# A vision tower on one core: the first attention step of the first head group written apart from the loop, in another order

## The reference

```python
h = _L0_tok_ref(...)                       # 8 batches x 256 tokens x 512, from a state space kernel
h = h + attn(_layernorm(h))                # 16 query heads, 4 key/value heads, 128 wide, window 256
h = h + ffn(_layernorm(h))                 # selected low-rank update per token

q, k, v = hidden @ w_q, hidden @ w_k, hidden @ w_v      # per head
q = q * cos + rotate_half(q) * sin                      # k likewise
probs = softmax(q @ k.T / sqrt(128) + causal_bias)
out = (probs @ v) @ w_o
```

## Time and profile before

| | |
|---|---|
| median of 3 runs | 835.1 us (834.56 to 835.16) |
| the profiled execution, its own time | 833.84 us |
| its span, first to last instruction | 832.0 us |
| PE busy | 753.5 us, 91% |
| DVE, ACT, POOL busy | 577.2, 454.5, 444.6 us |
| granted TensorE clock, mean | 0.974 |

### The profile page before, as it was taken

One profiled execution on the slowest core, in us unless ns is written; L12 is line 12 of the kernel. 1 busy time (PEld: TensorE's weight loads), 2 busy tenths in 40 slices (PEclk: granted clock), 3 DMA queues, 4 the chain that ended last, 5 costly groups with the idle time before them and its releaser, 6 DMA issues.

```text
span 832.0 us, 19710 instructions
## 1 busy us (share of the span) xinstructions
PE 753.5 (91%) x6958; PEld 685.6 (82%) x6958; DVE 577.2 (69%) x1626; ACT 454.5 (55%) x1246; POOL 444.6 (53%) x662
## 2 busy tenths in 40 slices
PE   0277877899999999999999999999999999999985
PEld 0176667899999999999999999999999989899762
DVE  7999648677766666656565566655655687777877
ACT  6644327555555656555575665555656554564420
POOL 0497826544444747444465654444747556555522
PEclk9998989899999999999999999999999999999995
DMA  9033450100010102000001020000100000000002
GB/s 208 0 67 63 86 218 27 39 1 0 0 39 2 52 1 77 0 0 0 0 8 45 10 68 0 0 0 0 52 2 1 1 2 26 25 25 25 1 25 77
DMA packets 30504, 26.48 MB, mean 32 GB/s; under 512 B 22446, under 2 KB 22830, under 8 KB 30198
## 3 DMA queue, kind: packets, MB, share of 16 engines
q1 hardware_dynamic: 30310, 25.77, 10.9%
q10 hardware_dynamic: 144, 0.07, 0.0%
HBM read 17.44 MB, written 8.39 MB: 31 GB/s over the span
## 4 chain that ended last, share of the span: by engine, by line
PE 77%; DVE 11%; POOL 5%; issue 3%; ACT 2%; DMA 1%; DVEq 0%; SPq 0%; POOLq 0%; ACTq 0%
PE bank_quad L1218 17%; PE bank_quad L1220 17%; PE bank_quad L1219 16%; PE bank_pair L1220 4%; PE bank_pair L1218 4%; PE bank_pair L1219 4%; POOL w_lo L423 2%; PE bank_pair L1361 2%; PE bank_pair L1371 1%; PE bank L1371 1%; PE bank L1375 1%; DVE bank_pair L905 1%; PE bank_quad L1314 1%; PE bank_quad L1230 1%; POOL kq_lo L493 1%
## 5 line engine op out<-in xcount | busy, mean ns | idle before, releaser
L1218 PE MATMUL bank_quad<-xt_hi,w_hi 128*128 (+1 forms) x768 | 217.2, 283 | 0.8 <-POOL w_lo L423 0.8
L1220 PE MATMUL bank_quad<-xt_lo,w_hi 128*128 (+1 forms) x768 | 214.9, 280 | 0.0
L1219 PE MATMUL bank_quad<-xt_hi,w_lo 128*128 (+1 forms) x768 | 214.8, 280 | 0.0
L987 DVE TENSOR_TENSOR kq<-bank_quad,cst 128x512 f32<-128x512 f32 (+1 forms) x96 | 57.9, 603 | 140.8 <-ACT swap L679 106.6
L489 POOL TENSOR_TENSOR swap<-swap,cst 128x512 f32<-128x512 f32 (+1 forms) x96 | 105.8, 1104 | 82.3 <-ACT swap L679 79.5
L1218 PEld LDWEIGHTS bank_quad<-xt_hi,w_hi 128*128 128x128 f32 x768 | 144.9, 189 | 2.8 <-POOL w_lo L423 1.4
L1220 PEld LDWEIGHTS bank_quad<-xt_lo,w_hi 128*128 128x128 f32 x768 | 144.7, 188 | 0.0
L1219 PEld LDWEIGHTS bank_quad<-xt_hi,w_lo 128*128 128x128 f32 x768 | 144.6, 188 | 0.0
L351 POOL TENSOR_TENSOR spare<-cst 1x1 f32<-1x1 f32 x87 | 16.6, 191 | 223.3 <-DVE rinv L1121 141.1
L719 ACT ACTIVATE sm<-sm,mx 128x128 f32<-128x128 f32 (+1 forms) x256 | 114.2, 447 | 21.5 <-DVE mx L1111 21.5
L678 ACT ACTIVATE swap<-bank_quad 64x512 f32<-64x512 f32 (+1 forms) x96 | 50.4, 524 | 125.1 <-PE bank_quad L1220 122.6
(11 more groups left out here) (265 smaller groups left out, 1883.2 us busy)
## 6 DMA issues: line engine op xcount, KB each, us to landing
mixed<-st SPq DMA_DIRECT2D x32, 128.0 KB, 2.0
out<-x SPq DMA_DIRECT2D x16, 256.0 KB, 2.0
raw<-in_w_qkv SPq DMA_DIRECT2D x8, 384.0 KB, 3.5
raw<-in_w_o SPq DMA_DIRECT2D x10, 256.0 KB, 2.7
x<-mixed SPq DMA_DIRECT2D x2, 1280.0 KB, 11.0
norm_mem<-in_w_qkv SPq DMA_DIRECT2D x6, 384.0 KB, 3.6
x<-mixed SPq DMA_DIRECT2D x3, 512.0 KB, 4.6
norm_mem<-in_w_o SPq DMA_DIRECT2D x6, 256.0 KB, 2.7
```

Of the source, the lines that this page charges most:

```text
L987: v.tensor_tensor(view(kq), src, table(cosT), ALU.mult).then_inc(kq_cos, 1)
L1218: mmul(dst, lh, rh, start=start and k == 0, stop=False, skip_group_check=True)
L1219: mmul(dst, ll, rh, start=False, stop=False, skip_group_check=True)
L1220: last = mmul(dst, lh, rl, start=False, stop=stop and k == n - 1, skip_group_check=True)
```

## The change

It takes the first run `(0, 1)` out of `RUNS[0]`, and so step 0 of group 0 out of the loop body, and writes it out on each engine ahead of `steps`; the exceptions for it in the step's functions are gone.

- PE: V of batch 0 is transposed into bank 7, between the two query pairs of batch 0, and waits only for `vt`. Keys and values of batch 1 are projected ahead of batch 0's scores. Behind the transposes of the probabilities stands one `keep_warm` matmul in bank 3, and V of batch 1 is transposed behind `attend(0)` instead of ahead of it.
- DVE: the statistics of batch 2 move ahead of the first query pair's cosine product; the low parts of keys and queries of batch 0 stand between the rotations. In step 0 the first reciprocals and V's low part come ahead of `norm_apply` for batch 2, and the statistics of batch 3 and the low parts of the probabilities come ahead of the second query pair of batch 1.
- ACT: the rounding of batch 0's parts and the first two chunks of `w_o` stand between the swaps; `swap(1, (0,))` is ahead of the exponents; the first two parts of batch 1 are rounded ahead of the probabilities.
- POOL: the norm of batch 2 comes ahead of the sine products of the queries, the sine product of batch 1's key ahead of the normalising, and low parts and the norm of batch 3 between the others. The last two chunks of `w_o` are split at the end of the step on ACT and POOL.

The core of the diff; helpers that were only cut into pieces (`rotate_sin`, `kq_rest`, `project_kv`, `project_q`, `turn_v`) are left out:

```diff
 RUNS = [
-    [(0, 1), (1, 2), (2, 5), (5, 6), (6, 7), (7, 8)],
+    [(1, 2), (2, 5), (5, 6), (6, 7), (7, 8)],
...
@@ POOL
-            rotate(0, rests=False)
+            rotate_sin(0, 0)
             norm(2)
+            rotate_sin(0, 1)
+            rotate_sin(0, 2)
             for n in (KC, KC + 1):
                 split_lo(n)
...
+            rotate_sin(1, 0)
+            normalise_probs(0)
+            rotate_sin(1, 1)
+            kq_rest(1, 0)
+            kq_rest(1, 1)
+            norm(3)
+            rotate_sin(1, 2)
+            kq_rest(1, 2)
+            for k in range(KC + 2, NCK):
+                split_lo(k)
             steps(pool, step)
...
@@ ACT
             xt1(1)
+            round_kq(0, (0,))
+            split_hi(KC)
             swap(0, (2,))
-            for n in (KC, KC + 1):
-                split_hi(n)
-            round_kq(0)
-            round_v(0)
+            round_kq(0, (1,))
+            split_hi(KC + 1)
+            round_v(0, 7)
+            round_kq(0, (2,))
+            swap(1, (0,))
...
+            exponents(0)
+            swap(1, (1,))
+            xt1(2)
+            round_kq(1, (0, 1))
+            round_probs(0)
+            swap(1, (2,))
+            round_kq(1, (2,))
+            round_attn(0)
+            round_v(1)
+            for k in range(KC + 2, NCK):
+                split_hi(k)
             steps(act, step)
...
@@ DVE
             rope(0, 0)
+            dve.wait_ge(x_third, 16)
+            norm_stats(tokens(2), 2)
             rope(0, 1)
             rope_add(0, 0)
             xt_rest(1)
+            rope_add(0, 1)
+            kq_rest(0, 0)
             rope(0, 2)
-            rope_add(0, 1)
+            kq_rest(0, 1)
             rope_add(0, 2)
...
+            kq_rest(0, 2)
...
+            masked_scores(0, True)
+            reciprocals(0, (0,))
+            v_rest(0, 7)
+            norm_apply(tokens(2), 2)
+            reciprocals(0, (1,))
+            rope(1, 0)
+            rope(1, 1)
+            rope_add(1, 0)
+            xt_rest(2)
+            rope_add(1, 1)
+            dve.wait_ge(x_rest, 32)
+            norm_stats(tokens(3), 3)
+            probs_rest(0)
+            rope(1, 2)
+            rope_add(1, 2)
+            norm_apply(tokens(3), 3)
+            attn_rest(0, 0)
             steps(dve, step)
...
@@ PE
-            project(0, 0, True, lambda: None, lambda: first_tokens(1))
-            transpose_v(0)
+            project_kv(0)
+            project_q(0, 0)
+            first_tokens(1)
+            pe.wait_ge(swapped, 1)
+            turn_v(7)
+            project_q(0, 1)
+            pe.wait_ge(xt_lo, 4)
+            pe.wait_ge(swapped, 1)
+            pe.wait_ge(kq_cos, 1)
+            project_kv(1)
...
+            scores(0, first=True)
+            pe.wait_ge(kq_cos, 2)
+            pe.wait_ge(swapped, 2)
+            project_q(1, 0)
+            pe.wait_ge(xn_ready, 3)
+            pe.wait_ge(s_masked, 4)
+            transpose_tokens(2)
+            project_q(1, 1)
+            pe.wait_ge(xt_lo, 6)
+            pe.wait_ge(v_lo, 1)
+            transpose_probs(0)
+            keep_warm(1, 3)
+            pe.wait_ge(swapped, 5)
+            pe.wait_ge(kq_cos, 5)
+            attend(0)
+            transpose_v(1)
             steps(pe, step)
```

More of the change, by code:

```diff
@@ L682, in swap, with round_kq @@
                     last.then_inc(swapped, 1)
-            def round_kq(s):
-                for j in range(3):
+            def round_kq(s, parts=range(3)):
+                for j in parts:
                     _, _, part, flat = rope_view(j)
@@ L1005, in _, with kq_rest @@
             norm_apply(tokens(1), 1)
+            def kq_rest(s, j):
+                _, _, part, flat = rope_view(j)
+                dve.wait_ge(kq_hi, s * 3 + (j + 1))
+                v.tensor_tensor(flat(kl), part(kq), flat(kh).bitcast(F32), ALU.subtract).then_inc(kq_lo, 1)
             rope(0, 0)
+            dve.wait_ge(x_third, 16)
+            norm_stats(tokens(2), 2)
             rope(0, 1)
@@ L1009, in _ @@
             xt_rest(1)
+            rope_add(0, 1)
+            kq_rest(0, 0)
             rope(0, 2)
-            rope_add(0, 1)
+            kq_rest(0, 1)
             rope_add(0, 2)
-            for j in range(3):
-                _, _, part, flat = rope_view(j)
-                dve.wait_ge(kq_hi, j + 1)
-                v.tensor_tensor(flat(kl), part(kq), flat(kh).bitcast(F32), ALU.subtract).then_inc(kq_lo, 1)
-            dve.wait_ge(x_third, 16)
-            norm_stats(tokens(2), 2)
+            kq_rest(0, 2)
             def add_output(i, b, tiles=range(TT)):
@@ L1116, in masked_scores, with reciprocals @@
                         attn_rest(i - 1, 1)
-                v_rest(i)
-            def reciprocals(i):
-                dve.wait_ge(p_exp, i * 4 + 2)
-                v.reciprocal(rinv[:, 0:4], rsum[:, 0:4]).then_inc(r_ready, 1)
-                dve.wait_ge(p_exp, i * 4 + 4)
-                v.reciprocal(rinv[:, 4:8], rsum[:, 4:8]).then_inc(r_ready, 1)
+                if not first:
+                    v_rest(i)
+            def reciprocals(i, halves=range(2)):
+                for k in halves:
+                    dve.wait_ge(p_exp, i * 4 + (2 * k + 2))
+                    v.reciprocal(rinv[:, 4 * k:4 * k + 4], rsum[:, 4 * k:4 * k + 4]).then_inc(r_ready, 1)
             def probs_rest(i):
@@ L1132, in step @@
                 i = b + 8 * g
-                masked_scores(i, g == 0 and at == 0)
-                if g == 0 and at == 0:
-                    norm_apply(tokens(2), 2)
+                masked_scores(i)
                 if needs_norm1(g, at):
-                    if at == 0:
-                        dve.wait_ge(x_rest, 32)
                     norm_stats(tokens(b + 3), b + 3)
@@ L1239, in lead, with keep_warm @@
                 mmul(banks[2 * s][:, 4 * P - 2:4 * P], pair(g1), pair(bt)[:, 0:2], start=True, stop=True, skip_group_check=True)
-            def keep_warm(count):
+            def keep_warm(count, bank=0):
                 for _ in range(count):
-                    mmul(banks[0][:], ident, cst[:, 0:512], start=True, stop=True)
+                    mmul(banks[bank][:], ident, cst[:, 0:512], start=True, stop=True)
             pe.wait_ge(cst_in, 16)
@@ L1306, in transpose_v @@
                 pe.wait_ge(kq_cos, s * 3 + 3)
-                for t in range(TT):
-                    last = nc.tensor.transpose(banks[2][:, t * P:(t + 1) * P], vt[:, t * P:(t + 1) * P], ident)
-                last.then_inc(vt_ready, 1)
+                turn_v(2)
             def gate_product(bb, bank=0):
@@ L1345, in _, with scores @@
             pe.wait_ge(xt_lo, 2)
-            project(0, 0, True, lambda: None, lambda: first_tokens(1))
-            transpose_v(0)
-            def scores(i, g, at):
+            project_kv(0)
[8 more added lines that the diff above has]
+            project_kv(1)
+            def scores(i, first=False, no_output=False):
                 pe.wait_ge(kq_lo, i * 3 + 2)
                 for j in range(QH):
-                    if j == 0 and (g or at > 1):
+                    if j == 0 and not (first or no_output):
                         pe.wait_ge(x_added, i * 2 - 2)
@@ L1390, in step @@
                 i = b + 8 * g
-                scores(i, g, at)
+                scores(i, no_output=g == 0 and at == 1)
                 def after_kv():
```

112 lines of the change are left out of this document (57 added, 55 removed).

## The result

The changed kernel takes 829.62 us (median of 4 runs, 828.27 to 830.31); the kernel before, beside it, 834.86 us (4 runs, 834.56 to 835.16). The ratio is 0.9940, with a 95% interval of 0.9926 to 0.9954: 5.2 us faster, where 4.7 were forecast, and 829.62 for a forecast of 830.4. The profiled execution of the changed kernel took 829.41 us, its span is 827.6. One later execution of the kernel before was in a slow state of its own, 1275.63 us at a mean clock of 0.57, and no ratio counts it.

The account below looks back on a forecast made before the run. PE's own work bounds the loop, a latency chain the stretch ahead. 3.9 + 2.0 + 0.6 − 0.2 = 6.3 us, minus 1.6 for a clock fall, gives 4.7 and a median of 830.4 us; range 828.0 to 833.3.

Parts of the forecast that it names:

- What bounds the kernel: Loop over groups and batches bound by PE's own work, so a microsecond gained ahead of 153 us moves the rest forward.
- The chain: Step-by-step walk from batch 0's projections to attend, which would start at 143.9 instead of 147.77: 3.9 us saved.
- Keys and values ahead: Batch 1's keys and values run from 125.0 to 128.0, ahead of batch 0's scores, out of PE's later path.
- The lock: DVE instructions with two SBUF inputs and POOL's SBUF reads exclude each other; without it the sum would be 0.9 us better.
- The table load: ACT's load ahead of batch 0's exponents loses its cover: 1.28 us, no drain; exponents no earlier than before.
- The clock terms: At clock 1.00 attend saves 2.0 us and the next scores 0.6; V's transposes behind attend give back 0.2.
- one fall in attend: PE's clock falls once in attend, after a 2.4 us wait, for 3.1 us: costs 1.6 us.
- rival 1: The warming matmul splits the idle time, so attend runs at 2.4 GHz: 6.3 us saved, 828.8 us; chance 0.30.
- The longer chain: Clock falls behind the 1.6 us wait for batch 2's tokens; attend near 147, 1.5 to 3.5 us saved; chance 0.15.
- the slower case: Clock falls ahead of batch 1's keys and stays down while waits recur: 4.7 us slower, 839.8 us; chance 0.04.
- What was costed at nothing: Earlier loads of chunks 6 and 7, the wait for remaining tokens, and ACT's and POOL's splits ahead of step 1: no cost.

Follow-up runs that it names:

- V in bank 2: The changed kernel with V of batch 0 transposed into bank 2 again, behind batch 1's keys and values; 828.98 us, ratio 0.9954 to the kernel before.
- table early: The changed kernel with an unused one-element exponential on ACT ahead of rounding batch 0's second query pair, loading the table earlier; 827.17 us.
- three warmings: The changed kernel with three warming matmuls instead of one ahead of attend; 829.03 us, ratio 0.9942 to the kernel before.
- split later: The changed kernel with POOL's splits of two w_o chunks moved behind the sine product of batch 1's key; 826.32 us.
- no warming: The changed kernel without the warming matmul behind the transposes of batch 0's probabilities; 829.71 us, ratio 0.9953 to the kernel before.
- both: The changed kernel with POOL's two w_o splits later and the exponent's table load early, together; 829.10 us, ratio 0.9941 to the kernel before.

## Why the prediction was right, and where it was off

**What bounds the kernel: right.** The loop passes a gain on one to one. Behind the scores of batch 1 all waits of PE up to 757 us are the three for POOL's `w_lo`, 0.8 us in all, as before.

**The chain, 3.9 us: right in its steps, 3.3 in size.** Shifted by the 1.1 us between the two traces, the walk gives 126.9 for the scores (measured 126.57), 131.0 for the first exponent (130.88), 134.6 for the tokens of batch 2 (134.24), 138.3 for the end of the last query pair (138.20), 142.8 for attend (143.34). Two terms were too small. POOL's normalising was costed at 1.64 us a half from the earlier trace rows, with DVE elsewhere; it took 2.07 and 1.79, in part beside DVE's `norm_apply`, and `rope_add(1, 1)` behind it ended 0.4 us late. And 0.26 us from the end of DVE's last low part to PE's start was left out, though the rows had it: 146.24 + 1.27 is 147.51, and attend began at 147.77. Smaller ones cancel: PE waits 1.50 us between the heads, not 1.0, since I gave the last low part 0.5 us and the split made it 0.93. Ahead of the tokens it waits 0.65 instead of 1.6, since it comes there 0.6 us later than in the walk and the tokens are ready 0.4 sooner.

**Keys and values ahead: right, and the largest part shown, but for more than the reason given.** Without them the median is 2.2 us higher and attend 3.93 us later in the trace, up to 2.85 of it by a fall of the clock that came only with the longer waits. The prediction did not name that: it laid the scores of batch 0 out at full clock, so that the 3.1 us at half of the earlier trace rows, some 1.6 us of PE's work, stood inside its 3.9 us. How much of them had reached attend no run shows. The new bank (0.26) and the reciprocals (0.38) are small beside it, which the prediction did not say apart.

**The lock: right,** 0.9 charged, 1.10 shown. **The table load: right,** 1.28 us on the path since the scores had become first, 0.90 of it visible at attend once removed. But the exponents do not come "no earlier than before", they come later. The prediction had them wait for the end of all scores at 132.2; in the trace before, the first waits only for the first head's row maxima:

```profile
130.88 0.41 ACT L719 ACTIVATE sm<-sm,mx 128x128 f32<-128x128 f32 x1 [1.13 <-DVE mx L1111]
```

That is 10.76 us behind the transposes of batch 1's tokens, and now it is 11.85 (119.03 to 130.88). The whole gain on the way to attend comes behind the exponents.

**The clock terms, 2.0 + 0.6 − 0.2: measured 1.8, 0.6 and −0.2.** Attend takes 2.18 us at 1.00, not half of 3.98. The first scores took back their 0.6; but one pass of the loop, between 421 and 441 us, now takes 0.3 us more (20.72 for 20.39), which no row explains. It need not belong to the new order, since three traces of it (V in bank 2, table early, three warmings) have this pass at 20.38 or 20.39; the cause stays open.

**The step that failed is "one fall in attend", −1.6 us.** The forecast let the clock fall; it did not, in both traces of the changed kernel. What happened is rival 1, the clock holds, with 5.25 us in the place of its 6.3. The forecast of 4.7 came near by luck: 1.6 us taken off for a fall that did not come met a gain 1.05 us too large elsewhere. I placed a wait of 2.4 us between 0.93 and 2.7 by its length alone. The runs show that at this length the length does not decide: at 2.75 us the clock held in three traces (the change twice, split later) and fell in two (V in bank 2, table early). The size of the term was right: a fall costs 1.54 us up to batch 3's tokens (no warming) or 1.56 (V in bank 2, less its 0.26 at attend), 1.25 of it in attend. A chance of one half would have fitted it, and the forecast would have been the same within 1 us. How often the clock falls there in the kernel before, which has one profile, is not known either, so the 2.4 us that the clock gives in this pair of traces are not shown to be in every run; the medians give 3.8 to 5.2 us for the whole.

**The other rivals.** The longer chain did not come: no fall behind the wait of 0.65 us. Nor did the slower case; the waits of 0.52, 1.50 and 0.65 us left the clock at 1.00. What was costed at nothing cost nothing: the earlier splits and loads show no wait of PE in step 1.

## What to carry to other kernels

In a latency chain ahead of a loop bound by TensorE, look for the work of the next item that is ready and put it where the engine waits; here it was the largest single piece, 2.2 us by the medians, and part of that is a clock that no longer falls in the shorter waits. A bank and the order of two small instructions paid 0.3 and 0.4 us; getting POOL's splits and the table load out of the way paid 1.1 and 0.9 at attend. Walk the chain with durations taken where both SBUF engines were busy, and add the hand-over from engine to engine. Two gains found apart need not add: after each, read again which wait ends last.

## What the hardware showed unexpectedly

- After the same wait of 2.75 us behind the same matmuls, the clock held at 1.00 through attend in the changed kernel, and fell in two variants, in one of them 0.6 us ahead of the first matmul (table early), in the other 0.9 us behind it (V in bank 2). With such a wait the clock can go either way; the five traces with 1.0 to 1.7 us there held it, and the three with 3.2 to 3.6 us (before, both, no warming) did not.
- Stretches of PE over the last 50 us of the two traces of the changed kernel:

```profile
776.00:827.00 51.00, 37.27 (x166) 26.56 (x166) 37.57 (x110) 10.21 (x28) 14.23 (x26) 0.81 0.11 42
```

```profile
776.00:827.00 51.00, 36.33 (x166) 24.74 (x166) 38.03 (x114) 11.10 (x33) 14.97 (x27) 0.85 0.12 42
```

The busy times are those of PE, its weight loads, DVE, ACT and POOL, and behind them stands the granted clock: 0.81 and 0.85 for the same 166 matmuls (the second trace stands 1.0 us later). The same code takes 49.4 to 51.6 us there, a spread wider than most parts of this change are worth. The mean clock alone does not sort them: counted from the landmark at the end of the loop, the second trace takes 51.37 us at 0.84, and the one with three warmings 50.21 at 0.85.
- The lock works on both sides: POOL's two splits took 3.15 us beside DVE's addition and 2.55 without it (splits later, both).
